# The tokenizer's products over 192 split as 128 and 64 rows, its biases added when its sums are read, and a new order of the work

## What is computed

```python
# a, tokenizer (per image: 64 tokens of 192, 12 heads of 16)
x = layernorm(patches(x) @ patch_w + patch_b) * g + b + positions
identity = x
x = gelu(x @ ff1_w + ff1_b) @ ff2_w + ff2_b          # 192 -> 768 -> 192
x = attention(x @ qkv_w + qkv_b) @ proj_w + proj_b + identity
x = gelu(x @ ff1_w + ff1_b) @ ff2_w + ff2_b + x      # the same weights again
h = concat(x, txt)                                   # 96 tokens
# end of a: normalised, a gated convolution block (in_proj, conv, out_proj)
# b: attention of 12 heads of 16, then 192 -> 768 -> 192 with gelu
# c: top-2 gates over 12 heads of 64, attention with normalised q, k, proj
```

## Time and profile before

| | us |
|---|---|
| median of 3 runs | 716.83 (716.1 to 717.5) |
| the profiled execution | 716.47 |
| its span, first to last instruction | 714.7 |

### The profile page before, as it was taken

The page is one execution under the profiler, slowest core; times in us unless marked ns, Lnnn a source line. Parts: engine busy times, 40 slices in busy tenths (PEclk is TensorE's granted clock), DMA queues, the critical chain, the costliest instruction groups (busy, mean ns, idle before and its releaser), DMA issues.

```text
span 714.7 us, 10713 instructions
## 1 busy us (share of the span) xinstructions
PE 629.8 (88%) x4198; PEld 439.3 (61%) x4198; DVE 423.3 (59%) x861; ACT 291.3 (41%) x365; POOL 58.8 (8%) x54
## 2 busy tenths in 40 slices
PE   4968769989998999989999999989999978898797
PEld 3646456666466586666566686767555755664465
DVE  3026553763578944763678935654778829414983
...
DMA packets 12345, 15.57 MB, mean 22 GB/s; under 512 B 6952, under 2 KB 10058, under 8 KB 11916
## 3 DMA queue, kind: packets, MB, share of 16 engines
...
...
## 4 chain that ended last, share of the span: by engine, by line
issue 71%; PE 12%; POOL 7%; DVE 7%; ACT 1%; DMA 1%; POOLq 0%; SPq 0%; DVEq 0%; ACTq 0%
POOL a_wide L1571 3%; PE ps L490 2%; POOL root L1553 2%; PE ps L742 1%; PE ps L493 1%; PE ps L482 1%; PE ps L516 1%; PE ps L483 1%; DMA x_in<-in_xT 1%; DVE ss L1473 1%; PE ps L621 1%; POOL hx L1601 1%; POOL hx L1593 1%; POOL hx L1591 1%; PE ps L929 1%
## 5 line engine op out<-in xcount | busy, mean ns | idle before, releaser
L490 PE MATMUL ps<-w_cqkv,bT 128*128 128x512 f32 (+1 forms) x136 | 64.6, 608 | 0.0
L1372 DVE TENSOR_REDUCE smax<-ps 96x12 f32<-96x1152 f32 x32 | 43.2, 1351 | 31.7 <-PE ps L787 27.8
L1065 ACT ACTIVATE pr<-pr 96x1152 f32<-96x1152 f32 x32 | 37.2, 1162 | 57.5 <-DVE pr L1374 57.4
L1382 DVE TENSOR_REDUCE psum<-pr 96x12 f32<-96x1152 f32 x32 | 43.0, 1343 | 12.7 <-ACT pr L1065 12.3
L1553 POOL TENSOR_TENSOR root<-root,minus_half 128x3 f32<-128x3 f32 (+1 forms) x16 | 15.6, 973 | 416.9 <-DVE root L1270 256.3
L797 PE MATMUL ps<-w_ident,pr 96*96 96x96 f32 x384 | 40.5, 259 | 6.4 <-DVE pr L1394 4.4
L797 PEld LDWEIGHTS ps<-w_ident,pr 96*96 96x96 f32 x384 | 35.1, 133 | 14.4 <-issue 9.1
L1374 DVE TENSOR_TENSOR pr<-ps,smax 96x1152 f32<-96x1152 f32 x32 | 43.3, 1353 | 1.1
L1071 ACT ACTIVATE pT<-ps 96x1152 f32<-96x1152 f32 x32 | 35.9, 1121 | 19.0 <-PE ps L797 19.0
L490 PEld LDWEIGHTS ps<-w_cqkv,bT 128*128 128x128 f32 (+1 forms) x136 | 24.9, 197 | 29.6 <-issue 28.1
L1098 ACT ACTIVATE scratch<-ps 128x1536 f32<-128x1536 f32 x12 | 17.4, 1451 | 54.1 <-PE ps L493 54.1
...
## 6 DMA issues: line engine op xcount, KB each, us to landing
...
```

The source lines that it names most:

```text
L490: pe.matmul(out_ap, lhs(n, 0, slice(0, 128)), rhs(n, 0, slice(0, 128)), start=True, stop=False)
L1065: act.activation(pr[:, s % 2, :], pr[:, s % 2, :], ACT.Exp, scale=head ** -0.5)\
L1372: dve.tensor_reduce(mx, t, AX.X, ALU.max).then_inc(S[stage + "_max"], 1)
L1382: dve.tensor_reduce(psum[:, s % 2, :], e, AX.X, ALU.add).then_inc(S[stage + "_sum"], 1)
```

## The change

Stage a is treated as b and c are. x0T, x1T, x2T, a_qT, a_kT and hT hold the 192 features as 128 rows and 64 rows (the second 64 doubled where a product sums over them), and w_tff1, w_tqkv and the positions are loaded in that layout.
- `a_f1` now makes all six blocks by two `split_product`s of three; `a_g1` is gone. Gelu is applied block by block with the bias, six times instead of three.
- `a_f2` sums into 128 outputs. `a_h2` sums into the other 64, the products of even and odd position going to PSUM partitions 0 to 63 and 64 to 127; DVE adds the two halves (two or three instructions instead of one).
- `a_qk` makes three blocks of 128, read by four ACT instructions with the bias. `a_v` sums over 128 rows, then over 64 rows, for each sample. `a_s` sums over 128 rows (8 heads, 512 columns) and over 64 rows (4 heads, 256 columns) for each sample.
- `a_x0` has six transposes instead of four; those of `a_ht` alternate between 128 and 64 rows.
- The v bias of the tokenizer is folded through w_tproj by a new unit, `a_tb`.
- SP's list of loads: 6 more under "vec", 6 "tcols", 2 more for "tff1", 14 more for "tqkv", 2 more for "tproj", 2 more for the text; the four of v_split moved from "cols" to "vec". All of these stand ahead of the loads of "cqkv", "cols", "in", "out", "qkv" and "proj".
- The three lists of units are new. The first section's is shown in full: `a_pb` now stands between `a_qk` and `a_s.0`, where it stood behind `a_ot.1`. Stages b and c compute what they did, with the same instructions.

```diff
+A_H_ORDER = (0, 2, 4, 1, 3, 5)
+A_PARTS = ((128, slice(0, 8)), (64, slice(8, 12)))
 PAIR_AT = {0: (0, 0), 1: (1, 0), 2: (2, 0), 4: (0, 1), 5: (1, 1), 3: (2, 1)}
-VB = {"ff1": 0, "q": 6, "k": 8, "n": 10}
+VB = {"ff1": 0, "q": 6, "k": 8, "tok_ff1": 10, "tok_q": 16, "tok_k": 18, "n": 20}
...
-    a_en a_em=3 a_x0=4 warm.0=0 a_f1.0=6 a_g1.0 a_f2.0=5 a_h2.0 a_qk=6 a_v a_s.0=5 a_s.1=6 a_e.0 a_pt.0=0 a_o.0
-    a_e.1 warm.1=0 a_pt.1=1 a_wc.0 a_ot.0 a_o.1=4 a_ot.1=6 a_pb=3 a_pr=6 a_f1.1=3 a_wc.1 a_wc.2 a_g1.1=5 a_wc.3
-    a_f2.1=4 a_h2.1=1 a_ht warm.2 warm.3 a_u=2 warm.4=1 a_in.0=3 a_in.1=1 a_out.0=7 a_out.1=0 a_out.2=3
+    a_em a_en a_x0=0 warm.0=1 a_f1.0=2 a_f2.0 a_h2.0=3 a_qk=0 a_e.0 a_pb a_s.0 warm.1 a_v=3 a_s.1=5 a_pt.0 a_e.1
+    a_o.0=3 a_pt.1 a_wc.0 a_tb a_ot.0 a_o.1=5 warm.2=2 a_ot.1=3 a_pr=3 a_wc.1 a_f1.1=5 a_wc.2 a_f2.1=3 a_h2.1=6
+    a_ht=4 a_u warm.3 a_wc.3 a_in.0=3 a_in.1=4 a_out.0=4 a_out.1=2 a_out.2
...
-        n_loads = {"patch": 1, "vec": 9, "tff1": 2, "tff2": 1, "tqkv": 2, "tproj": 2, "in": 4, "out": 1, "qkv": 16,
-                   "proj": 2, "ff1": 4, "ff2": 1, "cqkv": 7, "cproj": 6, "ident": 1, "cols": 10}
+                                               "proj", "ff1", "ff2", "cqkv", "cproj", "ident", "cols", "tcols")}
+        n_loads = {"patch": 1, "vec": 15, "tff1": 4, "tff2": 1, "tqkv": 16, "tproj": 4, "tcols": 6, "in": 4, "out": 1, "qkv": 16,
+                   "proj": 2, "ff1": 4, "ff2": 1, "cqkv": 7, "cproj": 6, "ident": 1, "cols": 6}
...
+            n = V96["n"]
+            sp.dma_start(v_split[0:HC, 0, :], vec96).then_inc(loads["vec"], 16)
+            sp.dma_start(v_split[HC:128, 0, 0:n - 1], vec96[0:128 - HC, 1:n]).then_inc(loads["vec"], 16)
+            for half in (0, 64):
+                sp.dma_start(v_split[half:half + 64, 1, 0:n - 1], vec96[128 - HC:HC, 1:n]).then_inc(loads["vec"], 16)
+            sp.wait_ge(s_pad, 2)
+            for dst, src in ((v128[:], vec128), (w_mask[0:HC, 0:6], mask), (w_mask[HC:128, 6:8], mask[0:128 - HC, 0:2]),
+                             (w_prio[:], prio), (w_patch_b[:], patch_b), (w_ff2_b[:], ffn2_b), (w_cproj_b[:], cproj_b)):
+                sp.dma_start(dst, src).then_inc(loads["vec"], 16)
             sp.dma_start(w_ident[:, :], ident).then_inc(loads["ident"], 16)
             def rows_and_bias(name, dst, src):
 
@@ -416,38 +420,46 @@
                         sp.dma_start(dst[dst_rows, part, to:to + n], src[src_rows, from_part, at:at + n])\
                           .then_inc(loads[name], 16)
 
-            rows_and_bias("tff1", w_tff1, tok_ff1)
+            def column(name, rows, at, src):
+
+                sp.dma_start(v_bias[0:rows, at:at + src.shape[0] // rows], src.rearrange("(c p) -> p c", p=rows),
+                             allow_slow_non_contiguous=True).then_inc(loads[name], 16)
+
+            def text(group):
+                for rows, part, src_rows, src_part in ((slice(0, HC), 0, slice(0, HC), 0),
+                                                       (slice(HC, 128), 0, slice(0, 128 - HC), 1),
+                                                       (slice(0, 64), 1, slice(128 - HC, HC), 1)):
+                    sp.dma_start(hT[rows, part, :, NI:N], txtT[group, src_rows, src_part]).then_inc(S["txt_in"], 16)
+
+            HEAD_PARTS = ((0, 0, D), (D, D + 128, 64), (D + 64, D, 128), (2 * D, 2 * D, D))
+            split_rows("vec", w_pe, peT)
+            column("tcols", 128, VB["tok_ff1"], tok_ff1[HC, 0, :])
+            split_rows("tff1", w_tff1, tok_ff1)
+            for name, at in (("tok_q", 0), ("tok_k", D)):
+                column("tcols", 128, VB[name], tok_qkv[HC, 0, at:at + 128])
+                column("tcols", 64, VB[name] + 1, tok_qkv[HC, 0, at + 128:at + D])
+            sp.dma_start(tok_v_bias_row[:, :, HC], tok_qkv[HC, 0, 2 * D:3 * D].rearrange("(c p) -> p c", p=HC),
+                         allow_slow_non_contiguous=True).then_inc(loads["tcols"], 16)
             sp.dma_start(w_tff2[:], tok_ff2).then_inc(loads["tff2"], 16)
-            rows_and_bias("tqkv", w_tqkv, tok_qkv)
-            rows_and_bias("tproj", w_tproj, tok_proj)
-            sp.dma_start(hT[:, :, :, NI:N], txtT[0]).then_inc(S["txt_in"], 16)
+            split_rows("tqkv", w_tqkv, tok_qkv, cols=HEAD_PARTS)
+            for rows in (slice(0, HC), slice(HC, HC + 1)):
+                sp.dma_start(w_tproj[rows, :, 0:D], tok_proj[rows]).then_inc(loads["tproj"], 16)
+                sp.dma_start(w_tproj[rows, :, D:256], tok_proj[rows, :, 128:D]).then_inc(loads["tproj"], 16)
+            text(0)
...
+            def bias_through(w, unit, bias_row, weight, load):
+
+                for sem_read, value in reads_before(w, unit):
+                    pe.wait_ge(sem_read, value)
+                t = slot(w, unit)
+                for name in load:
+                    pe.wait_ge(loads[name], 16 * n_loads[name])
+                for kc in range(2):
+                    m = pe.matmul(t[0:HC + 1, 0:weight.shape[2]], bias_row[:, kc, :], weight[0:HC, kc, :],
+                                  start=(kc == 0), stop=(kc == 1))
+                m.then_inc(fill_sem(w, unit), 1)
+
+            def a_pb(w, _):
+                bias_through(w, ("a_pb", 0), v_bias_row, w_proj, ("cols", "proj"))
+
+            def a_tb(w, _):
+                bias_through(w, ("a_tb", 0), tok_v_bias_row, w_tproj, ("tcols", "tproj"))
...
+                for first in range(2):
+                    split_product([t[:, n, first * TA:(first + 1) * TA] for n in range(3)],
+                                  lambda n, kc, r: w_tff1[r, kc, (2 * n + first) * 128:(2 * n + first + 1) * 128],
+                                  lambda n, kc, r: src[r, kc, :], fill_sem(w, ("a_f1", j)) if first else None)
...
+                    row = n % 2 * 64
+                    m = pe.matmul(t[row:row + 64, 0:TA], w_tff2[:, kc, 128:D], a_h[:, kc, :], start=(n < 2),
+                                  stop=(n >= F // 128 - 2))
...
-                for n in range(4):
-                    o = t[0:HC, n // 2, (n % 2) * TA:(n % 2 + 1) * TA]
-                    chunks(o, lambda kc, k: w_tqkv[0:k, kc, n * HC:(n + 1) * HC], lambda kc, k: x1T[0:k, kc, :],
-                           fill_sem(w, ("a_qk", 0)) if n == 3 else None)
+                split_product([t[:, n, 0:TA] for n in range(2)], lambda n, kc, r: w_tqkv[r, kc, n * 128:(n + 1) * 128],
+                              lambda n, kc, r: x1T[r, kc, :])
+                split_product([t[:, 0, TA:2 * TA]], lambda n, kc, r: w_tqkv[r, kc, 2 * 128:3 * 128],
+                              lambda n, kc, r: x1T[r, kc, :], fill_sem(w, ("a_qk", 0)))
...
                 for s in range(GS):
-                    for odd in range(2):
-                        chunks(t[64 * odd:64 * odd + NI, s * HC:(s + 1) * HC],
-                               lambda kc, k: x1T[0:k, kc, s * NI:(s + 1) * NI], lambda kc, k: wv[0:k, kc, odd],
-                               fill_sem(w, ("a_v", 0)) if s == GS - 1 and odd else None)
+                    tokens = slice(s * NI, (s + 1) * NI)
+                    for kc in range(2):
+                        for odd in range(2):
+                            rows = slice(64 * odd, 64 * odd + 64)
+                            r = rows if kc else slice(0, 128)
+                            m = pe.matmul(t[rows, s * HC:(s + 1) * HC], x1T[r, kc, tokens], wv[r, kc, odd],
+                                          start=(kc == 0), stop=(kc == 1))
+                m.then_inc(fill_sem(w, ("a_v", 0)), 1)
...
-                    for c in range(2):
-                        m = pe.matmul(t[64 * half:64 * half + NI, c, 0:6 * NI], a_qT[:, c, s * NI:(s + 1) * NI],
-                                      a_kB[:, c, :, half * NI:(half + 1) * NI], start=True, stop=True)
+                    for c, (rows, heads_of) in enumerate(A_PARTS):
+                        m = pe.matmul(t[64 * half:64 * half + NI, heads_of.start * NI:heads_of.stop * NI],
+                                      a_qT[0:rows, c, s * NI:(s + 1) * NI],
+                                      a_kB[0:rows, heads_of, half * NI:(half + 1) * NI], start=True, stop=True)
...
-                    for c in range(2):
-                        m = pe.transpose(t[:, tile, c * HC:(c + 1) * HC], hv[:, c, tile * 128:(tile + 1) * 128],
-                                         w_ident[0:HC, 0:HC])
+                    cols = slice(tile * 128, (tile + 1) * 128)
+                    pe.transpose(t[:, tile, 0:128], hv[:, 0, cols], w_ident[:, :])
+                    m = pe.transpose(t[:, tile, 128:D], hv[0:64, 1, cols], w_ident[0:64, 0:64])
...
-                t = slot(w, ("a_g1", j))
-                act.activation(a_h[:, 4:6, :], t.rearrange("p (c t) -> p c t", c=2), ACT.Gelu_apprx_tanh)\
-                   .then_inc(S["a_h"], 1)
+                if w.section == "first" and j == 0:
+                    act.wait_ge(loads["tcols"], 16 * n_loads["tcols"])
+                for c in A_H_ORDER:
```

(14 more changed lines are left out.)

261 lines of the change are left out of this document (113 added, 148 removed).

## The result

The changed kernel takes 810.12 us (median of four runs, 804.8 to 813.03), the kernel before beside it 716.47 us (715.69 to 717.5): a ratio of 1.129, 95% interval 1.125 to 1.133. The profiled execution is 810.24 us, its span 808.5. The forecast was 740, the range 723 to 755; the sign was right, the size was not: 94 us came where 24 were expected.

What follows compares the result with a forecast made beforehand. It took PE's work to bound the three passes and a chain of waits, loads included, the first section. 716.5 + 9.4 (passes) + 14.3 (first section) = 740.2 us, forecast 740, range 723 to 755.

Steps and rivals of the forecast that it cites:

- What bounds the kernel: Passes: PE's work sets the time; first section: the chain of waits, loads included; edits count by length there.
- The units on PE: Stage a's changed units at full clock: +3.1 us a group of four images, +9.4 us over three passes.
- rival 1: a_s's halves still run together and a_v's parts cost 0.27 us: passes -3 us, total 725; chance 0.17.
- Rival 3: Changes of rows hidden by weight loads running ahead, only slots count: -6.3 us a group, total 709; chance 0.07.
- Hidden in a pass ... 0 and +-2: In a pass, extra ACT and DVE instructions cost nothing; the new order changes PE's idle time by 0, +-2 us.
- The first section: a_pb waits for w_proj, landing at 53 (47.5 to 58.5): +13.3, then +2 and -1, sum +14.3 us.
- The last section: After the passes, only a new order of units: 0, +-3 us.
- Rival 4: New lists leave more of PE idle, or w_proj lands at 58: total 752 us; chance 0.13.

Runs made afterwards that it cites:

- e2_new_order: The kernel before with the changed kernel's new lists of units, a_g1 put right behind a_f1 and a_tb dropped; 768.8 us.
- e8_warm: The changed kernel with three more filler units (warm.6 to warm.8) in front of a_qk in the loop list; 773.5 us.
- e5_phases: The changed kernel under the three old lists, instructions inside a_f1, a_qk, a_v, a_s and a_ht reordered so that 128-row and 64-row parts stand together; 758.1 us.
- e4_h2_first: The changed kernel with a_h2.0 put ahead of b_s.2 and b_e.2 in the loop list; 803.8 us.
- e3_pb_late: The changed kernel with a_pb alone moved behind a_ot.1 in the first list; 803.9 us.
- the best form: The changed kernel under the old lists, with e5_phases' orders inside units and w_tqkv's and w_tproj's loads on ScalarE's queue; 750.8 us, ratio 1.048.

## Why the prediction was wrong, step by step

**What bounds the kernel.** "In the three passes the time is what PE has to do, so an edit counts by its length on PE." This reading of rows 2 was right for the kernel before (10.4 us idle, clock 0.98) and was carried over to a kernel with other lists, where it is false: 19.8 us idle and 0.91. The regrouped units show that length counts when the order stays; e2_new_order shows that order counts 17 us when length stays.

**The units on PE.** This part held. At full clock:

| unit | predicted | measured |
|---|---|---|
| a_f1 | 5.1 | 5.1 |
| a_h2 | 1.5 | 1.44 |
| a_qk | 3.0 | 2.85 |
| a_v | 2.9 | 2.5 |
| a_s | 3.4 | 3.15 |
| a_ht | 1.6 | 1.4 |

a_qk is taken from e8_warm, since in the changed kernel the clock falls inside it. The sum forecast +3.1 us a pass; e8_warm gives +2.5 for the work. The choice against rival 1, that a_s's two samples would not run beside each other, was right, and e5_phases showed the reason: it is the row count between them. Rival 3, changes of rows for nothing, is out.

**"Hidden in a pass ... 0 and +-2".** This is the step that failed: +21 a pass instead (23.4 less 2.5 of work), 9.4 of it idle time and 11.5 the clock behind it. The step had two parts. I put the evictions of ACT and DVE at nothing because these engines are busy for 47 and 64% of a pass. The share of busy time says nothing on where an eviction stands: DVE's x1T now has one more dependent step, behind the 2.7 us of b_s.2, with PE's a_qk directly behind. And I gave the new lists a symmetric 2 us, where they were the part that no row of the trace before could price. The lists alone cost 17 us; 13 us more of PE's idle time, with new waits of 3.2 us for c_kT, 3.2 in two for pr (0.7 before), 2.0 for b_kB (1.3 before) and one of 4.6 us that the trace puts down to no engine.

**The clock in the loop wasn't in the sum at all.** Rows 2 gave 0.98 in a pass, and I held it there. e8_warm put a number to it: about 11.5 us of the 23.4 a pass, 9.4 of them in the one stretch of 23.9 us. A gap can be paid twice, by its own length and by what runs at half clock behind it. It need not be: the longest wait of the pass, 3.2 us for c_kT, has only 3.4 us at half clock behind it, and in e4_h2_first the clock fell for 17.1 us although the wait of 2.7 us was gone.

**The first section.** The mechanism was right (a_pb waits for w_proj, SP's queue stands still once more before "in") and the size was not: w_proj was issued at 56.27 and used at 58.8, which is my upper bound of 58.5 and not the 53 I took. The assumption that failed is that a good part of the added issues vanishes in the pause: they took 17.1 us where I had 12 to 16, and the pause gave back 1.7. The terms, by the cut of the forecast (the loop's first instruction, 130.73 for 105.85, +24.9): a_s.0 begins at 60.30 for 41.09, +19.2 where I had +13.3. From there to the second a_f1 (85.15) it is 24.9 us for 23.6, +1.3 where I had +2. From there on it is 45.6 us for 41.2, +4.4 where I had -1; the waits for u are 1.4 us longer there, and the stretch behind the second a_f1 has a clock of 0.80 where it had 0.89. With w_proj at 58.5 the forecast would have been 19.8. e3_pb_late showed the wait to be only the first in a line: a_pb moved away brings 6.3 us, not 21.9, because DVE then waits for w_cproj.

**The last section.** 0 came out (0.1), with luck: the same work took 123.8 to 133.5 us in the other runs.

**Rival 4** ("the new lists leave more of PE idle, or w_proj lands at 58: 752") named both mechanisms and was priced 12 us above the forecast where 70 came. Both happened, and a stretch at half clock lay beside each.

What stays open: why the clock comes back after 3.4 to 6.8 us behind some gaps of 1 to 3 us and after 23.9 behind that one, at the same place in three passes. Of the idle time that is left in the best form (17.2 us in its second pass for 10.4) the trace names the places: waits of 2.8 us for c_kT, 1.7 for hT, 1.6 for gelu ahead of b_v, and 1.3 and 1.1 at a_h2.0 and a_f2.0 for evictions by ACT, none of them there before. Which instruction of the change makes each of them was not tested, nor was a list made for the regrouped units.
